# A two-layer graph network on one core: bulk units, the query drain, the x1 loads and PSUM banks rearranged, with constant matmuls in the softmax

## The reference

```python
h = jnp.maximum(_layernorm(x), 0.0)
x = x + relu(segment_sum(w[:, None] * (h @ W)[src], dst))       # layer 0
h = jnp.maximum(_layernorm(x), 0.0)                              # layer 1, 8 heads of 32
score = einsum('ehd,ehd->eh', (h @ Wq)[dst], (h @ Wk)[src]) / sqrt(32)
score = score + relu(efeat @ W1 + b1) @ W2 + b2
alpha = segment_softmax(score, dst)
out = segment_sum(alpha[:, :, None] * (h @ Wv)[src], dst)
return x + out @ Wo + bo
```

## Time and profile before

| | |
|---|---|
| three runs | 870.81, 874.93, 875.78 us (median 874.93) |
| the profiled execution | 874.82 us, of which its span 872.9 us |
| mean granted TensorE clock | 0.934 of full speed |
| busy: PE, DVE, ACT, POOL | 686.4, 570.7, 473.2, 503.1 us |
| moved by DMA | 224 MB, mean 257 GB/s |

### The profile page before, as it was taken

How to read it: one execution, slowest core, us unless ns; L and a number is a source line. 1 busy time by engine, 2 the same in 40 slices (tenths; PEclk the granted TensorE clock), 3 DMA queues, 4 the chain that set the end, 5 groups by cost and what they waited for, 6 DMA issues and landing times.

```text
span 872.9 us, 13157 instructions
## 1 busy us (share of the span) xinstructions
PE 686.4 (79%) x3704; PEld 532.6 (61%) x3704; DVE 570.7 (65%) x1673; ACT 473.2 (54%) x1385; POOL 503.1 (58%) x432
## 2 busy tenths in 40 slices
PE   1376888999999999856999999999941358888883
PEld 0244665666666677635878888888831246666662
DVE  5278887888888876302676655555578248888883
ACT  0437786788888888622434444444452547555520
POOL 5888888788888851027566666553021105777663
PEclk9997999999999999986999999999975579999998
DMA  7877999999999984836388988979779995556551
GB/s 227 266 259 231 306 318 314 315 343 342 345 347 339 341 271 153 284 110 208 119 284 293 298 280 296 300 254 325 270 214 289 249 348 162 169 191 200 181 174 49
DMA packets 122937, 224.00 MB, mean 257 GB/s; under 512 B 27461, under 2 KB 100800, under 8 KB 112882
## 3 DMA queue, kind: packets, MB, share of 16 engines
q1 hardware_dynamic: 75602, 148.73, 50.9%
q0 software_dynamic: 21280, 48.73, 18.8%
q10 hardware_dynamic: 25984, 25.69, 8.4%
HBM read 133.05 MB, written 102.76 MB: 270 GB/s over the span
## 4 chain that ended last, share of the span: by engine, by line
PE 56%; DVE 16%; DMA 12%; issue 6%; ACT 4%; POOL 3%; ACTq 1%; DVEq 0%; SPq 0%; POOLq 0%
PE bank L1000 48%; DMA q<-ringC 4%; DVE small L984 4%; DMA ringB<-x 3%; PE bank L1115 2%; DVE store L973 2%; ACT ringB L609 2%; PE bank L1096 2%; DVE ringA L964 2%; PE bank L1069 1%; DMA h<-ringB 1%; DVE pz L765 1%; PE bank L1175 1%; POOL ringA L456 1%; DVE small L786 1%
## 5 line engine op out<-in xcount | busy, mean ns | idle before, releaser
L456 POOL DMA_INDIRECT store<-h,slot_gather x98 | 134.5, 1372 | 117.6 <-PE bank L1115 65.9
L1000 PE MATMUL bank<-Wkv_sb,small 128*128 128x256 f32 x784 | 187.1, 382 | 1.7 <-issue 1.7
L1000 PEld LDWEIGHTS bank<-Wkv_sb,small 128*128 128x128 f32 x784 | 150.5, 192 | 22.5 <-issue 2.1
L1000 PE MATMUL bank<-Wo_sb,small 128*128 128x256 f32 x392 | 108.1, 400 | 45.5 <-DVE store L973 45.5
L876 DVE TENSOR_TENSOR work<-bank,msgs 128x256 f32<-128x256 f32 x98 | 41.3, 422 | 133.8 <-PE bank L1000 133.8
L506 POOL DMA_INDIRECT out_x<-store,out_scatter x98 | 97.2, 991 | 52.0 <-issue 36.9
L456 POOL DMA_INDIRECT ringC<-in_x,dst_gather x98 | 92.6, 945 | 44.8 <-issue 25.7
L664 ACT ACTIVATE ringA<-store,scores 128x32 f32<-128x32 f32 x392 | 87.1, 309 | 48.9 <-PE bank L1175 45.8
L1000 PE MATMUL bank<-Wq_sb,small 128*128 128x256 f32 x392 | 104.8, 391 | 8.9 <-ACT ringC L537 8.8
L637 ACT COPY store<-bank 128x256 f32<-128x256 f32 x98 | 36.5, 372 | 134.7 <-PE bank L1000 134.7
L1000 PEld LDWEIGHTS bank<-Wo_sb,small 128*128 128x128 f32 x392 | 68.9, 196 | 61.5 <-DVE small L984 36.0
(11 more groups left out here) (180 smaller groups left out, 1249.6 us busy)
## 6 DMA issues: line engine op xcount, KB each, us to landing
out_x<-bulk SPq DMA_DIRECT2D x32, 1152.0 KB, 10.3
bulk<-in_x SPq DMA_DIRECT2D x28, 1152.0 KB, 8.0
ringA<-q SPq DMA_DIRECT2D x14, 896.0 KB, 7.0
ringB<-x SPq DMA_DIRECT2D x14, 896.0 KB, 5.4
out_x<-ringC SPq DMA_DIRECT2D x9, 1152.0 KB, 9.6
ringC<-in_x SPq DMA_DIRECT2D x7, 1152.0 KB, 8.0
x<-ringB SPq DMA_DIRECT2D x14, 512.0 KB, 3.7
h<-ringB ACTq DMA_DIRECT2D x14, 512.0 KB, 9.3
```

Of the source, the lines that this page charges most:

```text
L456: pool.indirect_dma_start(to, None, table, bass.IndirectOffsetOnAxis(ap=at, axis=0), **more).then_inc(landed, 16)
L1000: return nc.tensor.matmul(o, lhsT, rhs, start=start, stop=stop)
```

## The change

Seven things. Bulk units 0 to 13 move two turns later, behind the edge inputs on SP, and ACT runs one square root at its start (ramp). The query chain trails by J + 4 = 11 tiles in place of 14; the last tiles alternate between banks 0 and 4, and the last group's q goes to the lower half of ringC, without the wait for `st_q` (q drain). The first two q loads are issued before the open row is stored; its row is then loaded separately into ringA's last partition, and GpSimd gathers four tiles ahead of fetching it, not two. The attention loop takes 24 bulk units in place of 21, in another order on SP. The first two x1 loads go from SP to ACT, behind its last fills, and wait for the last use of the masks in ringB. `project` uses four banks. TensorE multiplies `ident` by `Wosb` into bank 6 before six waits of the softmax, 50 times in all; nothing reads the results.

```diff
+IDLE = (10, 4, 16, 5, 12, 3)
+LAG = J + 4
+LAST_Q = T - LAG - 1
-MIDDLE = EARLY + 3 * G // 2
+MIDDLE = EARLY + 24
...
+        def q_bank(t):
+            return bank[0 if t > LAST_Q and (t - LAST_Q) % 2 else 4]
+        def q_row(l, j):
+            return C(j if l == G - 1 else J + j)
+        def units(g):
+            k = MIDDLE - EARLY
+            return range(EARLY + k * g // G, EARLY + k * (g + 1) // G)
...
 # SP, edges
-                if g + 2 < EARLY:
-                    bulk_load(g + 2)
                 if on(-1):
...
+                if 0 <= g < EARLY:
+                    bulk_load(g)
                 if on(1):
                     rows_out(x1r, st_x[1][lb], x1_d, ringB, 1, 1, lb)
-                if 0 <= g + 1 < EARLY:
-                    bulk_store(g + 1)
+                if 0 <= g - 1 < EARLY:
+                    bulk_store(g - 1)
...
 # SP, behind the edge loop
             bulk_load(EARLY + 1)
+            sp.wait_ge(h1, T)
+            for i in range(2):
+                sp.wait_ge(st_q[i], 32)
+            for a in range(2):
+                q_in(a)
+            for a in range(2):
+                sp.wait_ge(ql[a], 16)
             sp.wait_ge(open_in, 16)
             sp.dma_start(q_d...[:, P - 1, :], q_open).then_inc(open_out, 16)
+            sp.wait_ge(open_out, 16)
+            sp.dma_start(ringA[P - 1:P, :]..., q_d...[P - 1:P, 0:2 * J, :]).then_inc(open_to, 16)
             bulk_load(EARLY + 2)
-            sp.wait_ge(open_out, 16)
-            for a in range(2):
-                q_in(a)
...
 # SP, attention loop
-            for u in range(EARLY, MIDDLE):
...
+            for g in range(G):
+                for u in units(g):
+                    bulk_store(u)
+                    if EARLY < u < MIDDLE - 2:
+                        bulk_load(u + 2)
+                if g + 2 < G:
+                    sp.wait_ge(same_rdy, g + 1)
+                    ends_in(g + 2)
+                    sp.wait_ge(qs, J * (g + 1))
+                    q_in(g + 2)
-            for u in range(MIDDLE, MIDDLE + 4):
+            for u in range(MIDDLE, BULK + 1):
                 bulk_store(u)
 # SP, attend: x1 loads of groups 2 to 13 only, the later bulk stores gone
...
 # GpSimd
-                    if j == 3 and 0 <= g + 2 < EARLY:
+                    if j == 3 and 0 <= g < EARLY:
...
-                if t == 2:
+                if t == 4:
...
 # ACT
+            act.wait_ge(pdve, 1)
+            nc.scalar.activation(ssum[0:1, 0:1], epsc[0:1, :], ACT.Sqrt)
...
-                    if j == 1 and on(3):
-                        rows_out(q2, st_q[1], q_d, ringC, l3, 1, 1)
-                    if j == 5 and on(2):
-                        rows_out(q2, st_q[0], q_d, ringC, l2, 0, 1)
+                    if j in (2, 5) and on(2):
+                        rows_out(q2, st_q[j // 3], q_d, ringC, l2, j // 3, 0 if l2 == G - 1 else 1)
...
-            for u in range(MIDDLE + 4, MIDDLE + 6):
+            for u in range(MIDDLE + 4, BULK + 1):
                 fill(u)
+            act.wait_ge(rb_free, 1)
+            for a in range(2):
+                act.dma_start(group(ringB, a), edge_rows(x1_d, a)).then_inc(x4[a], 16)
             act.wait_ge(al_ps, 5)
...
 # VectorE, pairs
-                    if j == 2:
-                        add_unit(EARLY + g + g // 2)
-                    if j == 5 and g % 2:
-                        add_unit(EARLY + g + g // 2 + 1)
+                    if j in (2, 5) and j // 3 < len(units(g)):
+                        add_unit(units(g)[j // 3])
...
 # TensorE
-                    need(pe, q2, t)
+                    need(pe, q2, t if t <= LAST_Q + 1 else t - 1)
-                        ins = mm(bank[4][:, 0:D], hT[v % 2][:, c, :], Wqsb[:, c, :],
+                        ins = mm(q_bank(t)[:, 0:D], hT[t % 2][:, c, :], Wqsb[:, c, :],
...
+                        pe.wait_ge(open_to, 16)
...
+            def idle_work(n):
+                for _ in range(n):
+                    mm(bank[6][:, 0:D], ident[:, :], Wosb[:, 0, :])
             for k in range(2):
+                idle_work(IDLE[2 * k])
                 pe.wait_ge(pe_sm, 2 * k + 1)
...
+                idle_work(IDLE[2 * k + 1])
                 pe.wait_ge(pe_sm, 2 * k + 2)
...
+                    idle_work(IDLE[4 + j // 4])
                     pe.wait_ge(pe_sm, 5 + j // 4)
...
-                    need(pe, o4, t - 1)
+                    need(pe, o4, t - 3)
-                        mm(bank[2 + v % 2][:, 0:D], aT[v % 2][:, c, :], Wosb[:, c, :], start=(c == 0), stop=False)
+                        mm(bank[2 + t % 4][:, 0:D], aT[v % 2][:, c, :], Wosb[:, c, :], start=(c == 0), stop=False)
```

More of the change, by code:

```diff
@@ L424, in attend @@
                         flags_in(a)
-                    if a == 0:
-                        sp.wait_ge(pe_sm, 5)
-                    need(sp, o4, J * (a - 1))
-                    sp.dma_start(group(ringB, ab), edge_rows(x1_d, a)).then_inc(x4[ab], 16)
-                if g == 0:
-                    for u in range(MIDDLE + 4, MIDDLE + 6):
-                        bulk_store(u)
+                        need(sp, o4, J * (a - 1))
+                        sp.dma_start(group(ringB, ab), edge_rows(x1_d, a)).then_inc(x4[ab], 16)
             turns(attend, ahead=1, behind=0)
@@ L519, in edges @@
                 l2, _, l2b = behind(2, g, h, b)
-                l3, _, l3b = behind(3, g, h, b)
                 def message(j):
@@ L530, in message, with copy_q @@
                                          scale=wcol[:, t:t + 1]).then_inc(msg_rdy, 1)
-                def copy_q(l, lb, j):
-                    act.wait_ge(qp, J * l + j + 1)
+                def copy_q(t):
+                    l, j = t // J, t % J
+                    act.wait_ge(qp, t + 1)
                     for part, (lo, _) in enumerate(PARTS):
-                        if j == lo:
+                        if j == lo and l < G - 1:
                             need(act, st_q[part], 16 * l)
-                    nc.scalar.copy(C(J + j), bank[4][:, 0:D]).then_inc(q2, 1)
+                    nc.scalar.copy(q_row(l, j), q_bank(t)[:, 0:D]).then_inc(q2, 1)
                 def hidden(half, c):
@@ L582, in edges @@
                     message(j)
-                    if on(2):
-                        u = l2b * J + j
-                        act.wait_ge(t2, J * l2 + j + 1)
-                        need(act, qp, J * l2 + j - 1)
-                        nc.scalar.copy(hT[u % 2], bank[3][:, 0:D].rearrange("p (c e) -> p c e", c=NC)).then_inc(hT2, 1)
-                    if j == 0 and on(3):
-                        copy_q(l3, l3b, J - 1)
-                    if j > 0 and on(2):
-                        copy_q(l2, l2b, j - 1)
+                    t = J * g + j - LAG
+                    if 0 <= t < T:
+                        act.wait_ge(t2, t + 1)
+                        need(act, qp, t - 1)
+                        nc.scalar.copy(hT[t % 2], bank[3][:, 0:D].rearrange("p (c e) -> p c e", c=NC)).then_inc(hT2, 1)
+                    if 0 < t <= T:
+                        copy_q(t - 1)
                     if 1 <= j and on(-1):
@@ L658, in _ @@
             for t in range(1, T, 2):
-                if t in (3, 5, 9):
-                    fill(MIDDLE + {3: 6, 5: 7, 9: 8}[t])
                 need(act, ag4, t - 2 * J + 1)
@@ L938, in both_scans @@
                 sm.link(nc.vector.tensor_copy(carry[:, :], bank[3][0:GH, 0:2]))
-                for i in range(2):
-                    sm.link(nc.vector.scalar_tensor_tensor(fwd, reach[i], carry[:, i:i + 1], fwd, o0, o1))
+                sm.link(nc.vector.scalar_tensor_tensor(fwd, reach[0], carry[:, 0:1], fwd, o0, o1))
+                ins = nc.vector.scalar_tensor_tensor(fwd, reach[1], carry[:, 1:2], fwd, o0, o1)
+                if is_max:
+                    sm.link(ins)
+                else:
+                    ins.then_inc(rb_free, 1)
+                    dve.wait_ge(rb_free, 1)
             both_scans(xs, True)
```

47 lines of the change are left out of this document (16 added, 31 removed).

## The result

The changed kernel takes 815.41 us (median of 4 runs, 811.63 to 817.12) beside 874.08 us (median of 4, 870.81 to 875.78) for the kernel before: ratio 0.9327, 95% interval 0.9284 to 0.937. The forecast was 813 us. The profiled execution is one of 815.25 us with a span of 813.1 us, 59.8 us under the span of before.

A forecast was written before the change was run, and what follows sets the result against it. Bounds: DMA, TensorE and GpSimd in the edge loop, a serial drain, TensorE in the attention loop, then full DMA before the scatters. Terms -14 - 14 + 3 - 37 = -62 took 874.8 to 813 us, range 797 to 840.

The forecast's parts named there:

- Ramp (-14): Early edge loop: GpSimd's adds leave the first turns' fetches, 14 us less, with ends of -8 and -20.
- the forecast's lower end: Ramp: -20 us if the two early q landings lose most of what they take beyond three tiles of room.
- the edge loop doesn't move: Edge loop: DMA at 0.99 paces it and early turns grow by the ramp's gain; 827 us, chance 0.10.
- Drain (-14): Between edge and attention loops: serial chain of 28.6 us in place of 43.9, taken as -14, from -7 to -17.
- the 28 named as the sign: Sign of being right: the attention loop begins 28 us sooner, near 373 us.
- three query tiles less ahead of it on ACT bring it to 15.5: Drain: the last h2 store lands 15.5 us behind the last edge tile's point in place of 18.4.
- Attention loop (+3): Attention loop: 24 bulk units in place of 21 cost 3 us, from 0 to +8; DMA share about 0.87.
- The bound from the fullest turn of before: Attention loop: a two-unit turn moves 6.8 MB, 19.9 us at the fullest such turn's 342 GB/s, against 16.7.
- The rival of the paced loop: Attention loop paced by DMA: 842 us, or from 830 us on; chance 0.10, and 0.03 for slower than before.
- Softmax and last loop (-37): After the attention loop: three units fewer (28.0 us), earlier scatters, adds keeping ahead; -37 us, from -41 to -27.
- late adds: Last loop: x1 load still takes 28 us, 820 us; second form, tiles keep 1.59 us, 830 us; chance 0.20.
- Constant matmuls (0): Softmax: fifty matmuls shorten it by some 3 us, but bulk stores set the first scatter, so 0 counted.

The follow-up runs named there:

- E1: The changed kernel with bulk units 0 to 13 (loads, stores and GpSimd's adds) put back two turns earlier: 822.12 us.
- E4: The changed kernel without the fifty matmuls of constants: 817.55 us.
- E6: The changed kernel with queries 14 tiles behind in place of 11, and ACT's q stores placed as in the kernel before: 815.05 us.
- E11: E10 with each bulk add of GpSimd in the edge loop cut into three adds of three rows, fetches between them: 798.20 us.
- E7: The changed kernel with the open row stored before both whole q loads, and fetched by GpSimd behind two gathers: 815.58 us.
- E10: The changed kernel with 12 bulk units in edge-loop turns 0 to 11, 27 in the attention loop, whose first two loads go in turns 12 and 13: 802.00 us.
- E2: The changed kernel with 21 bulk units in the attention loop in place of 24, the last three filled and stored in the last loop: 848.24 us.
- E3: The changed kernel with the projections back in two banks: 838.40 us.
- E8: The changed kernel with the bulk loads of the attention loop's first two units issued behind the landing of the q loads: 815.03 us.
- E12: E11 with the q rows of a group stored in parts of 3, 2 and 2 tiles in place of two: 797.21 us.

## Why the prediction was right

**Ramp (-14).** Right in size and mechanism: E1 gives 12.7 us for the bulk units alone, between two executions without a long hold of pz. That the table has 12.7 us as well, for the whole edge loop, is a coincidence: without the hold it is 18.1 us (357.8 less the 339.7 of E4). The other 5.4 us (357.8 less the 352.4 of E1, where the units stand as before) lie in two turns of the kernel before that are 25.7 and 25.5 us apart, 22.7 and 22.2 in E1. That is what the forecast's lower end expected of the two early q landings, but their cause is open: E6, with lag and q stores as before, has no such turns, and in the kernel before they fall where the held operation changes from nm1 (up to 133.79 us) to pz (from 156.31 us), so it may have lost there what the changed kernel loses in its turn of 29.4 us. GpSimd is the engine without a pause in the steady turns: the adds of E4 are 22.5 us apart, those of E11 22.7, and the x1 stores keep that step. What I missed is that VectorE's small operations are held while GpSimd's add runs. The rival "the edge loop doesn't move" fell.

**Drain (-14).** Here a step failed, and by much: 7.8 us of gain, not 14. Counted from the first matmuls behind the last edge tile (344.75 us) to the landing of the open row (381.1) it is 36.4 us, not 28.6, and the attention loop began 20.5 us sooner (12.7 and 7.8), not the 28 named as the sign. The step that failed is "three query tiles less ahead of it on ACT bring it to 15.5": GpSimd's first gather comes 23.7 us behind that point (368.40 less 344.75). Two errors make up the 8.2 us. The store is issued 12.8 us behind the point in both kernels, as ACT does one query tile in each step, and the smaller lag takes away tiles behind the store, not ahead of it; E6 shows the same (0.4 us). ACT's timeline of the kernel before has the store that answers to the 357.50 us above:

```profile
370.15 0.37 ACTq L568 DMA_DIRECT2D h<-ringB  x1
```

That is 12.8 us behind the 357.39 of the earlier trace rows, and 5.6 us ahead of the first gather of the earlier trace rows. After, the store took 10.04 us to land, because the q loads and two bulk loads were in flight beside it. I had that sharing in the sum at 1 us. E7 takes 2.9 us of it away with the q loads, E10 5.4 with the bulk loads. The steps behind the gathers were right: fetch 2.7, store 1.7, load 2.46.

**Attention loop (+3).** Nothing of it came: 232.5 us with 21 and 24 units, 232.5 to 233.1 with 27. The bound from the fullest turn of before was too careful. The rival of the paced loop fell with room to spare, as 326 GB/s at a share of 0.91 shows (E10).

**Softmax and last loop (-37).** 38.8 us. The three units (28.0) were worth 30.9 (E2), the scatters followed at 1.30 us and not 1.28, and the pace of the adds was 1.275 us a tile, not 1.35. The landing of the x1 load was mis-sized: 20.10 us where I took 15. The adds began at 668.98 us, 51.0 us behind the last copy of v where the plan had 47 (686 less 639), and the faster tiles made up for it. E3 shows how near the rival "late adds" was by its second form: with two banks the adds set the end at 838 us, for which I had worked out 830.

**Constant matmuls (0).** Right on the path (E4). The 3 us of a shorter softmax were 0.8, because most of it is VectorE's own work, and the clock is lost again before the last loop.

## What to carry to other kernels

When a store stands at the end of a serial chain, look at what else is in flight at that moment, and move that work to before the drain begins, as E10 did; inside the drain E8 only found it another store to delay. A bulk operation that is cheap on an idle engine can be dear to its neighbour: look at the longest duration of each small operation, not only at its mean. And where an execution's stages shift by more than an edit is worth, compare stage by stage, not whole times.

## What had not been expected

Small VectorE operations were held until GpSimd's add had ended, up to 5.74 us (pz, in E2) where they take 0.17. In the 14 traces pz, nm1 and nm2 (the same of the second norm) are held for more than 0.8 us 146 times in the edge loop, and each time they end 0.03 to 0.04 us behind an add. Only some operations are held: pz (one tensor in SBUF, the engines' shared memory, and two constants), nm1 and, in E11 and E12, nm2 (two SBUF tensors each), never the additions that read a PSUM bank, nor the reciprocal of the same seven numbers (one SBUF tensor), which stays at 0.20 us or less beside the add as well. The holds that begin behind the start of an add, as most do, agree with a rule of the Trainium skill, "SBUF — State Buffer", Who interferes with whom: GpSimd shares a pair of ports with VectorE, and whichever of a GpSimd operation and a VectorE operation that needs the pair comes first keeps it to its end. The longest, over 5.1 us, don't, taken by the starts in the profile: in the changed kernel pz came 0.49 us ahead of the add (206.76 and 207.25) and was held all the same. Either such a start is not the moment at which the pair is taken, or the rule does not hold for these; no run shows which.

The cost of such a hold depended on where it fell. In E4 nm1 took 3.0 to 4.7 us in 11 of its 14 turns, and its loop ended with the earliest; one hold of pz of 5.58 us in the changed kernel came with a turn of 29.4 us. After it nm1 was held no more: the two engines had shifted against each other. The times of the changed kernel and of E4 to E8 fall into two groups with 3.6 to 5.7 us between them in each (E8: 811.5 to 812.2 and 817.9 to 820.3). The traces bear out the hold as the cause as far as one trace a kernel can: the changed kernel's was from the upper group and has the hold, the five of E4 to E8 from the lower and have no hold of pz over 1.9 us.
